# Decoder layer on one core: first output projection, residual, norm and cross-attention queries in one phase that also prepares the key and value weights

## The chip, the cores and the metric

The kernel runs on one core of a Trainium2 chip. The metric is the device time of one execution in microseconds. The core has a matrix engine (TensorE, PE; its weight loads are PEld), a vector engine (VectorE, DVE), a scalar engine (ScalarE, ACT), GpSimd (POOL) and a queue that issues most DMAs (SyncE, SP; SPq in the profile). Line numbers (L356) are those of the kernel before.

## The reference

A decoder layer on 4 sequences of 1024 tokens, width 512, 16 heads, with a context of 2048 tokens:

```python
x = x + attn(layernorm(x), q_heads, k_heads, v_heads, output_proj)      # causal; ends in out @ output_proj.T
x = x + xattn(layernorm(x), ctx, W_q, W_k, W_v, W_o, b_o)               # Q = (..) @ W_q, K = ctx @ W_k, V = ctx @ W_v
x = x + ffn(layernorm(x), gate_W, ..., W1, ..., W2, ...)                # the two best of 4 experts per token
```

## The kernel before

The layer is a row of phases. Each is a block with one instruction stream per engine; all engines meet at its end. The order of the work is written out by hand, and semaphores tie the streams together. The phases: qkv1, self attention, **out1** (`project_out`: attention @ output_proj.T plus residual, stored as x1), **q2** (`project`: x1 is loaded again, normalised, times W_q), **kv2** (`project`: context times W_k and W_v), cross attention, `finish` (last projection, norm, gates), experts.

Tokens go in chunks of 512: eight in out1 and q2, sixteen in kv2. A full-precision product is made of three fast ones: an operand is split into a high part (ACT, a copy to the fast type) and a low part (DVE, the difference), and hi*hi, hi*lo, lo*hi are added up in one PSUM bank. With four slices of the inner width that is 12 matmuls for 128x512 results, here called a tile (of the projection) or a query group.

`load_weights` (L74) loads the weights of a phase, turns them on PE if they are transposed (out1), and splits them in a block of its own; the phase's main block starts when it is over. In `project_out` (L924) a_in, a_hi, a_lo, res and y have two buffers each and the products four PSUM banks. In `project` (L136) DVE makes the statistics of a chunk (L258, L263, L266), POOL the inverse root (L243), DVE the normalised chunk (L273); PE turns it in four pieces (L356, "a turn": four transposes), ACT and DVE split these (L324, L279); PE multiplies (L373; L376 for values), ACT and DVE split the results (L336, L290), SP stores them. The four turns of the next chunk stand between the query groups of this one. x_in has two buffers, and a load goes out when its buffer has been normalised (L153).

`finish` (L1054), which the change leaves alone, has a projection of the same kind (L1463, with two bias matmuls more per tile, L1465 and L1466), with one buffer for a_hi and a_lo (L1285, L1347), two PSUM banks, adds at L1353, statistics from L1326, normalisation on ACT (L1271) and turns at L1479.

## Time and profile before

| | us |
|---|---|
| median of 3 timed runs | 4533.93 (4533.02 to 4535.35) |
| profiled execution | 4499.94 |
| its span | 4498.2 |
| PE, PEld, DVE, ACT, POOL busy | 4079.3, 2522.1, 2722.7, 2096.6, 2476.6 |
| out1, q2, kv2 begin (first DMA issue) | 1084.52, 1198.76, 1347.47 |
| cross attention begins | 1756.16 |

A timeline row has the start, the length, the engine, the line and operation with its output and inputs, how many follow each other, and in brackets the idle time before it with what ended it. In a row of groups the numbers are busy time, mean ns of one, then idle time before and its releasers. In a row of stretches they are the length, the busy time of each engine with its instructions, the granted clock of PE as a share of 2.4 GHz, the share of DMA time, and GB/s. Matmuls overlap, so the distance of starts is the pace, not one matmul's length.

### The profile page before, as it was taken

How to read it: one execution, taken by the hardware profiler on the slowest of the kernel's cores; microseconds unless marked ns; L12 is line 12 of the kernel's file. 1: busy time of each engine (PE TensorE's matmuls, PEld its weight loads, DVE VectorE, ACT ScalarE, POOL GpSimd, SP SyncE). 2: the span in 40 equal slices, each digit the busy share in tenths (PEclk: the TensorE clock that was granted, in tenths of full speed). 3: DMA queues.
4: the chain of work that ended last, by engine and by line, in shares of the span. 5: the costliest groups of instructions: out<-in, count | busy, mean ns of one | idle time of the engine just before them, and what ended most of it. 6: DMA issues, size and time to landing. Idle time of an engine off the chain costs nothing. (4 is left out here: it accounts for less than half of the span.)

```text
span 4498.2 us, 61641 instructions
## 1 busy us (share of the span) xinstructions
PE 4079.3 (91%) x21970; PEld 2522.1 (56%) x21970; DVE 2722.7 (61%) x4947; ACT 2096.6 (47%) x3870; POOL 2476.6 (55%) x931
## 2 busy tenths in 40 slices
PE   6998999997788998999999999999999967549997
PEld 5874555554667886444444444444444346438886
DVE  4436777773453334777777777777777333326765
ACT  2112555554122110566666666666666533226665
POOL 0002334332000001799999999999999915518887
PEclk8996999998899997999999999999999977669998
DMA  4546453522555556022222222222222056134444
GB/s 145 177 155 147 100 109 86 112 47 87 206 189 181 178 171 169 23 57 57 57 58 57 58 58 57 57 58 58 57 57 57 6 189 122 38 99 81 80 83 63
DMA packets 275065, 432.72 MB, mean 96 GB/s; under 512 B 31689, under 2 KB 132041, under 8 KB 268618
## 3 DMA queue, kind: packets, MB, share of 16 engines
q1 hardware_dynamic: 251050, 390.23, 32.6%
q0 software_dynamic: 19776, 36.85, 4.8%
q8 instruction: 161, 2.64, 0.3%
q10 hardware_dynamic: 3968, 2.10, 0.2%
q14 instruction: 110, 0.90, 0.1%
HBM read 258.57 MB, written 170.52 MB: 95 GB/s over the span
## 5 line engine op out<-in xcount | busy, mean ns | idle before, releaser
L881 DVE TENSOR_REDUCE cross_neg_max<-cross_scores 128x1 f32<-128x512 f32 x2048 | 1264.7, 676 | 397.0 <-PE cross_scores L708 396.9
L665 POOL TENSOR_TENSOR cross_partial<-cross_partial,cross_probs 128x2048 f32<-128x2048 f32 x320 | 1465.6, 4580 | 66.7 <-ACT cross_probs L832 29.5
L832 ACT ACTIVATE cross_probs<-cross_shifted 128x512 f32<-128x512 f32 x2048 | 1074.1, 606 | 748.0 <-PE cross_shifted L720 713.8
L708 PE MATMUL cross_scores<-cross_k_stack,cross_q_stack 96*128 96x512 f32 x2048 | 875.6, 437 | 39.5 <-DVE cross_neg_max L881 27.5
L720 PE MATMUL cross_shifted<-cross_q_stack,cross_k_stack 98*128 98x512 f32 x2048 | 850.7, 420 | 15.2 <-DMA cross_q_stack<-cross_neg_dram 6.7
L720 PEld LDWEIGHTS cross_shifted<-cross_q_stack,cross_k_stack 98*128 98x128 f32 x2048 | 387.1, 190 | 388.6 <-issue 239.9
L708 PEld LDWEIGHTS cross_scores<-cross_k_stack,cross_q_stack 96*128 96x128 f32 x2048 | 395.1, 193 | 286.6 <-DVE cross_neg_max L881 224.4
L832 ACT ACTIVATE self_probs<-self_shifted 128x512 f32<-128x512 f32 (+3 forms) x768 | 358.5, 492 | 366.2 <-PE self_shifted L723 285.3
L881 DVE TENSOR_REDUCE self_neg_max<-self_scores 128x1 f32<-128x512 f32 (+3 forms) x768 | 388.2, 547 | 207.1 <-PE self_scores L708 109.5
L736 PE MATMUL cross_out<-cross_probs,cross_v 128*32 128x512 f32 x4096 | 497.2, 603 | 0.0
L708 PE MATMUL self_scores<-self_k_stack,self_q_stack 96*128 96x512 f32 (+3 forms) x768 | 308.6, 423 | 21.7 <-DMA self_k_stack<-k_hi 10.0
L720 PE MATMUL self_shifted<-self_q_stack,self_k_stack 98*128 98x512 f32 (+3 forms) x768 | 298.9, 408 | 11.8 <-issue 11.0
L647 POOL MEMSET cross_neg_max<- 128x128 f32 x1 | 0.2, 210 | 440.9 <-POOLq L1842 440.9
L736 PEld LDWEIGHTS cross_out<-cross_probs,cross_v 128*32 128x32 f32 x4096 | 107.3, 109 | 232.4 <-issue 177.3
L720 PEld LDWEIGHTS self_shifted<-self_q_stack,self_k_stack 98*128 98x128 f32 x768 | 150.9, 198 | 110.8 <-issue 102.6
L663 POOL TENSOR_TENSOR cross_partial<-cross_probs 128x2048 f32<-128x2048 f32 x32 | 146.6, 4580 | 113.6 <-ACT cross_probs L832 113.6
L665 POOL TENSOR_TENSOR self_partial<-self_partial,self_probs 128x2048 f32<-128x2048 f32 (+1 forms) x32 | 128.4, 4014 | 123.1 <-ACT self_probs L832 123.1
L671 POOL TENSOR_TENSOR self_mixed<-self_out_sb,self_inv 128x512 f32<-128x512 f32 x32 | 40.8, 1274 | 281.2 <-issue 281.2
L708 PEld LDWEIGHTS self_scores<-self_k_stack,self_q_stack 96*128 96x128 f32 x768 | 159.6, 208 | 49.3 <-DVE self_neg_max L881 30.0
L1229 POOL DMA_INDIRECT lists<-finish_pairs,finish_place x128 | 134.6, 1051 | 85.2 <-issue 43.4
L901 DVE RECIPROCAL cross_inv<-cross_sum_sb 128x64 f32<-128x64 f32 x256 | 136.7, 539 | 68.4 <-ACT cross_sum_sb L818 68.4
L1724 ACT ACTIVATE experts_t<-experts_t,experts_neg_mean,experts_rstd 128x512 f32<-128x512 f32 x140 | 106.6, 808 | 96.3 <-DVE experts_neg_mean L1801 96.3
(271 smaller groups left out, 6241.5 us busy)
## 6 DMA issues: line engine op xcount, KB each, us to landing
cross_k_stack<-k_hi SPq DMA_DIRECT2D x30, 1024.0 KB, 20.4
kv_x_in<-in_ctx SPq DMA_DIRECT2D x16, 1024.0 KB, 5.5
k_hi<-kv_out_hi SPq DMA_DIRECT2D x64, 256.0 KB, 2.6
k_lo<-kv_out_lo SPq DMA_DIRECT2D x64, 256.0 KB, 3.2
v<-kv_out_n SPq DMA_DIRECT2D x64, 256.0 KB, 2.3
cross_v<-v SPq DMA_DIRECT2D x32, 512.0 KB, 25.1
self_q_stack<-q_hi SPq DMA_DIRECT2D x30, 512.0 KB, 6.9
self_k_stack<-k_hi SPq DMA_DIRECT2D x30, 512.0 KB, 15.6
```

What stands on the lines that cost most here:

```text
L647: pool.memset(neg_max[:, :, :, :], 3.0e38).then_inc(filled.sem, 1)
L663: nc.gpsimd.tensor_tensor(total, probs[:, (e - 1) % PB, :, :], own, ALU.add).then_inc(pool_added.sem, 1)
L665: nc.gpsimd.tensor_tensor(total, total, own, ALU.add).then_inc(pool_added.sem, 1)
L671: nc.gpsimd.tensor_tensor(mixed[:, q % 2], out_sb[:, q % 2], inv[:, :], ALU.mult).then_inc(scaled.sem, 1)
L708: mm = nc.tensor.matmul(scores[at][:, 0:width], q_st[0:96, w, h, q0:q0 + P], k_st[0:96, w, h, half * WIDE:half * WIDE + width], start=True ...
L720: mm = nc.tensor.matmul(shifted[n % SHIFTED][:, f:], k_st[0:98, w, h, kt * P:(kt + 1) * P], q_st[0:98, w, h, qb * QB + f:(qb + 1) * QB], s ...
L736: mm = nc.tensor.matmul(out_ps[32 * h:32 * h + 32, f:], v_sb[:, w, kt, 32 * h:32 * h + 32], probs[:, e % NE % PB, h, f:], start=kt == 0, s ...
L832: nc.scalar.activation(probs[:, e % NE % PB, h, f:], shifted[n % SHIFTED][:, f:], ACT.Exp).then_inc(exped.sem, 1)
L881: nc.vector.tensor_reduce(neg_max[:, q % 2, column(a), half:half + 1], scores[n % (SLOTS * ROUNDS) % AHEAD][:, 0:width], AX.X, ALU.max, ne ...
L901: nc.vector.reciprocal(inv[:, cols], sum_sb[:, cols]).then_inc(inverted.sem, 1)
L1229: pool.indirect_dma_start(lists, bass.IndirectOffsetOnAxis(place[:, t, e:e + 1], 0), pairs[:, t, e, :], None).then_inc(listed, 16)
L1724: nc.scalar.activation(dst[:, t], dst[:, t], ACT.Identity, scale=rstd[:, n, t:t + 1], bias=neg_mean[:, n, t:t + 1]).then_inc(ready, 1)
```

## The change

out1, q2 and the weight part of kv2 become one phase, `bridge`. x1 is stored and stays in SBUF for the norm. a_hi, a_lo, xt_hi, xt_lo have one buffer each, x_in three; the projection has two PSUM banks instead of four. Normalisation moves from DVE to ACT. W_k and W_v are loaded and split in the phase, behind chunks 2 and 4, and `project` takes them ready made; its two first x loads are then the first thing that SP does in kv2. The loops of the two phases become straight code. The helper `after` waits only for values above zero. "Iteration c" is pass c of the loop over the eight chunks; the projections of chunks 0 and 1 stand ahead of it.

```diff
-def project(nc, name, src, chunks, norm, weights, outs, ident, neg_half):
+def project(nc, name, src, chunks, norm, weights, outs, ident, neg_half, split=None):
...
-        load_weights(nc, f"{name}_w", weights, w_hi, w_lo, ident, first_loads)
+        if not split:
+            load_weights(nc, f"{name}_w", weights, w_hi, w_lo, ident, first_loads)
...
+            if split:
+                first_loads(sp)
...
-def project_out(nc, name, attn_t, weight, bias, residual, out, ident):
...
+def bridge(nc, name, attn_t, out_w, residual, x1, q_w, q_out, q_scale, next_w, next_hi, next_lo, ident, neg_half):
...
         a_in = sb("a_in", [P, 2, KT, CH])
+        a_hi = sb("a_hi", [P, KT, CH], F32R)
+        a_lo = sb("a_lo", [P, KT, CH], F32R)
+        x_in = sb("x_in", [P, 3, TPC, D])
+        xt_hi = sb("xt_hi", [P, KT, CH], F32R)
+        xt_lo = sb("xt_lo", [P, KT, CH], F32R)
+        turned = [ctx.enter_context(nc.psum_tensor(f"{name}_turned{n}", [P, KT, P], F32)) for n in range(2)]
+        acc = [ctx.enter_context(nc.psum_tensor(f"{name}_acc{n}", [P, D], F32)) for n in range(2)]
+        q_acc = [ctx.enter_context(nc.psum_tensor(f"{name}_q_acc{n}", [P, CH], F32)) for n in range(HG)]
...
         @block.sync
+            def load_attention(c):
+                after(sp, a_lo_ready, c - 1)
+                sp.dma_start(a_in[:, c % 2], attn_v[c // 2, :, :, c % 2 * CH:(c % 2 + 1) * CH]).then_inc(a_loaded[c % 2], 16)
+            def load(c):
+                if c >= 3:
+                    sp.wait_ge(x_stored[c % 3], 16 * (c // 3))
+                    sp.wait_ge(normed, TPC * (c - 2))
+                sp.dma_start(x_in[:, c % 3], tiles_of(residual)[c]).then_inc(loaded[c % 3], 16)
+            sp.dma_start(raw[:, 0], weight_rows(out_w)).then_inc(raw_loaded[0], 16)
+            load_attention(0)
+            load(0)
+            sp.dma_start(raw[:, 1], weight_rows(q_w)).then_inc(raw_loaded[1], 16)
+            load_attention(1)
+            load(1)
+            load_attention(2)
+            load(2)
+            sp.wait_ge(ow_lo_ready, KT)
+            sp.dma_start(raw[:, 0], weight_rows(next_w[0])).then_inc(raw_loaded[0], 16)
+            sp.wait_ge(qw_lo_ready, 1)
+            sp.dma_start(raw[:, 1], weight_rows(next_w[1])).then_inc(raw_loaded[1], 16)
+            for c in range(CHUNKS):
+                sp.wait_ge(added, TPC * (c + 1))
+                sp.dma_start(tiles_of(x1)[c], x_in[:, c % 3]).then_inc(x_stored[c % 3], 16)
+                if c + 3 < CHUNKS:
+                    load_attention(c + 3)
+                    load(c + 3)
+                for n in range(HG):
+                    sp.wait_ge(out_lo_ready, HG * c + n + 1)
+                    tok = slice(c % 2 * CH, (c % 2 + 1) * CH)
+                    for part, src in ((0, out_hi), (1, out_lo)):
+                        sp.dma_start(q_out[part][c // 2 * HG + n, :, tok], src[:, n].bitcast(F32)).then_inc(q_stored[n], 16)
...
         @block.scalar
+            def attention_high(c):
+                act.wait_ge(a_loaded[c % 2], 16 * (c // 2 + 1))
+                after(act, acc_ready, TPC * c)
+                nc.scalar.activation(a_hi[:, :, :], a_in[:, c % 2], ACT.Copy).then_inc(a_hi_ready, 1)
+            def normalise(c):
+                act.wait_ge(scaled, c + 1)
+                after(act, turned_ready, TPC * (c - 1))
+                for t in range(TPC):
+                    nc.scalar.activation(x_n[:, c % 2, t], x_in[:, c % 3, t], ACT.Identity, scale=rstd[:, t:t + 1],
+                                         bias=shift[:, t:t + 1]).then_inc(normed, 1)
+            def next_high(m):
+                act.wait_ge(raw_loaded[m], 32)
+                nc.scalar.activation(next_hi[:, m], raw[:, m], ACT.Copy).then_inc(next_hi_ready, 1)
...
+            attention_high(0)
+            act.wait_ge(raw_loaded[1], 16)
+            nc.scalar.activation(qw_hi[:, :, :], raw[:, 1], ACT.Copy).then_inc(qw_hi_ready, 1)
+            attention_high(1)
+            normalise(0)
+            attention_high(2)
+            for c in range(CHUNKS):
+                after(act, q_ready, HG * c)
+                for t in range(TPC):
+                    act.wait_ge(turned_ready, TPC * c + t + 1)
+                    nc.scalar.activation(xt_hi[:, :, t * P:(t + 1) * P], turned[t % 2][:, :, :], ACT.Copy).then_inc(hi_ready, 1)
+                if c + 1 < CHUNKS:
+                    normalise(c + 1)
+                if c + 3 < CHUNKS:
+                    attention_high(c + 3)
+                if c in (2, 4):
+                    next_high(c // 2 - 1)
+                for n in range(HG):
+                    act.wait_ge(q_ready, HG * c + n + 1)
+                    after(act, q_stored[n], 32 * c)
+                    nc.scalar.activation(out_hi[:, n], q_acc[n][:, :], ACT.Copy, scale=q_scale).then_inc(out_hi_ready, 1)
         @block.vector
...
+            def attention_low(c):
+                dve.wait_ge(a_hi_ready, c + 1)
+                nc.vector.tensor_tensor(a_lo[:, :, :], a_in[:, c % 2], a_hi[:, :, :].bitcast(F32), ALU.subtract).then_inc(a_lo_ready, 1)
+            def add_projection(c, t):
+                if t == 0:
+                    dve.wait_ge(loaded[c % 3], 16 * (c // 3 + 1))
+                dve.wait_ge(acc_ready, TPC * c + t + 1)
+                nc.vector.tensor_tensor(x_in[:, c % 3, t], acc[t % 2][:, :], x_in[:, c % 3, t], ALU.add).then_inc(added, 1)
+            def variance(c):
+                dve.wait_ge(added, TPC * (c + 1))
...
+            def scales(c):
+                dve.wait_ge(rooted, c + 1)
...
+            def next_low(m):
...
+            attention_low(0)
+            dve.wait_ge(qw_hi_ready, 1)
+            nc.vector.tensor_tensor(qw_lo[:, :, :], raw[:, 1], qw_hi[:, :, :].bitcast(F32), ALU.subtract).then_inc(qw_lo_ready, 1)
+            for t in range(TPC):
+                add_projection(0, t)
+            attention_low(1)
+            variance(0)
+            scales(0)
+            for t in range(TPC):
+                add_projection(1, t)
+            attention_low(2)
+            for c in range(CHUNKS):
+                for t in range(TPC):
+                    dve.wait_ge(hi_ready, TPC * c + t + 1)
+                    nc.vector.tensor_tensor(xt_lo[:, :, t * P:(t + 1) * P], turned[t % 2][:, :, :],
+                                            xt_hi[:, :, t * P:(t + 1) * P].bitcast(F32), ALU.subtract).then_inc(lo_ready, 1)
+                    if t == 0 and c + 1 < CHUNKS:
+                        variance(c + 1)
+                    if t and c + 2 < CHUNKS:
+                        add_projection(c + 2, t - 1)
+                if c + 1 < CHUNKS:
+                    scales(c + 1)
+                if c + 2 < CHUNKS:
+                    add_projection(c + 2, TPC - 1)
+                if c + 3 < CHUNKS:
+                    attention_low(c + 3)
+                if c in (2, 4):
+                    next_low(c // 2 - 1)
+                for n in range(HG):
+                    dve.wait_ge(out_hi_ready, HG * c + n + 1)
+                    after(dve, q_stored[n], 32 * c)
+                    nc.vector.scalar_tensor_tensor(out_lo[:, n], q_acc[n][:, :], q_scale, out_hi[:, n].bitcast(F32),
+                                                   ALU.mult, ALU.subtract).then_inc(out_lo_ready, 1)
         @block.tensor
+            def project_tile(c, t):
+                if t == 0:
+                    pe.wait_ge(a_lo_ready, c + 1)
+                after(pe, added, TPC * c + t - 1)
+                i = 0
+                for part, w in ((a_hi, ow_hi), (a_hi, ow_lo), (a_lo, ow_hi)):
+                    for k in range(KT):
+                        mm = nc.tensor.matmul(acc[t % 2][:, :], part[:, k, t * P:(t + 1) * P], w[:, k, :], start=i == 0, stop=i == 11)
+                        i += 1
+                mm.then_inc(acc_ready, 1)
+            def turn_tile(c, t):
+                pe.wait_ge(normed, TPC * c + t + 1)
+                after(pe, lo_ready, TPC * c + t - 1)
+                for k in range(KT):
+                    mm = nc.tensor.transpose(turned[t % 2][:, k, :], x_n[:, c % 2, t, k * P:(k + 1) * P], ident[:, :])
+                mm.then_inc(turned_ready, 1)
+            def queries(c, n):
+                after(pe, out_lo_ready, HG * (c - 1) + n + 1)
+                i = 0
+                for w, part in ((qw_hi, xt_hi), (qw_hi, xt_lo), (qw_lo, xt_hi)):
+                    for k in range(KT):
+                        mm = nc.tensor.matmul(q_acc[n][:, :], w[:, k, n * P:(n + 1) * P], part[:, k, :], start=i == 0, stop=i == 11)
+                        i += 1
+                mm.then_inc(q_ready, 1)
...
+            for t in range(2 * TPC):
+                project_tile(t // TPC, t % TPC)
+            for c in range(CHUNKS):
+                for t in range(TPC):
+                    turn_tile(c, t)
+                    if t and c + 2 < CHUNKS:
+                        project_tile(c + 2, t - 1)
+                if c + 2 < CHUNKS:
+                    project_tile(c + 2, TPC - 1)
+                pe.wait_ge(lo_ready, TPC * (c + 1))
+                if c == 0:
+                    pe.wait_ge(qw_lo_ready, 1)
+                for n in range(HG):
+                    queries(c, n)
...
-        in_phase(nc, project_out, "out1", attn1, (a["L0_attn_output_proj"], True), None, x, x1, ident)
-        in_phase(nc, project, "q2", x1, 2, True, [(a["L0_xattn_W_q"], False)], [("T", q2[0], q2[1], scale)], ident, neg_half)
-        in_phase(nc, project, "kv2", ctx_in, 4, False, [(a["L0_xattn_W_k"], False), (a["L0_xattn_W_v"], False)],
-                [("T", k2[0], k2[1], 1.0), ("N", v2)], ident, neg_half)
+        with ExitStack() as weights:
+            kv_hi = weights.enter_context(nc.sbuf_tensor("kv2_w_hi", [P, 2, KT, D], F32R))
+            kv_lo = weights.enter_context(nc.sbuf_tensor("kv2_w_lo", [P, 2, KT, D], F32R))
+            kv_w = (a["L0_xattn_W_k"], a["L0_xattn_W_v"])
+            in_phase(nc, bridge, "bridge", attn1, a["L0_attn_output_proj"], x, x1, a["L0_xattn_W_q"], q2, scale, kv_w, kv_hi, kv_lo, ident, neg_half)
+            in_phase(nc, project, "kv2", ctx_in, 4, False, [(w, False) for w in kv_w], [("T", k2[0], k2[1], 1.0), ("N", v2)],
+                     ident, neg_half, (kv_hi, kv_lo))
```

On PE, before, in q2: a turn, a query group, a turn, a query group (out1 was a phase of its own).

```order
L356 MATMUL q_turned<-ident,q_x_n 128x128 x4
L365 REGISTER_ALU
L373 MATMUL q_acc<-q_xt_hi,q_w_hi 128x512 x4
L373 MATMUL q_acc<-q_xt_hi,q_w_lo 128x512 x4
L373 MATMUL q_acc<-q_xt_lo,q_w_hi 128x512 x4
```

On PE now, at the head of iteration 1 of `bridge` (the names of acc are the projection's, of q_acc the queries'; the lines are the new kernel's).

```order
L1180 MATMUL bridge_turned<-ident,bridge_x_n 128x128 x8
L1172 MATMUL bridge_acc<-bridge_ow_hi,bridge_a_hi 128x512 x4
L1172 MATMUL bridge_acc<-bridge_ow_lo,bridge_a_hi 128x512 x4
L1172 MATMUL bridge_acc<-bridge_ow_hi,bridge_a_lo 128x512 x4
L1180 MATMUL bridge_turned<-ident,bridge_x_n 128x128 x4
L1172 MATMUL bridge_acc<-bridge_ow_hi,bridge_a_hi 128x512 x4
```

The turns now stand between tiles of the projection two chunks ahead, and a chunk's query groups follow its own turns. On DVE, before, in q2: statistics of a chunk two ahead between splits.

```order
L290 SCALAR_TENSOR_TENSOR q_out_lo<-q_acc,q_out_hi 128x512
L256 ISA
L258 BN_STATS q_stats<-q_x_in 128x6 x4
L260 ISA
L263 BN_AGGR q_mean_var<-q_stats 128x2 x4
L265 REGISTER_ALU
L266 TENSOR_SCALAR q_var_eps<-q_mean_var 128x4
L278 REGISTER_ALU
L279 TENSOR_TENSOR q_xt_lo<-q_turned,q_xt_hi 128x4x128
```

On DVE now, the head of iteration 0.

```order
L1143 TENSOR_TENSOR bridge_xt_lo<-bridge_turned,bridge_xt_hi 128x4x128
L1108 BN_STATS bridge_stats<-bridge_x_in 128x6 x4
L1112 BN_AGGR bridge_mean_var<-bridge_stats 128x2 x4
L1115 TENSOR_SCALAR bridge_var_eps<-bridge_mean_var 128x4
L1143 TENSOR_TENSOR bridge_xt_lo<-bridge_turned,bridge_xt_hi 128x4x128
L1103 TENSOR_TENSOR bridge_x_in<-bridge_acc,bridge_x_in 128x512
L1143 TENSOR_TENSOR bridge_xt_lo<-bridge_turned,bridge_xt_hi 128x4x128
```

The statistics now stand between the splits of the first and second turned piece, and the projection's adds behind the later ones.

## Rows read from the trace of the kernel before

**Rows 1.** Stretches: length; PE, PEld, DVE, ACT, POOL busy; granted clock, DMA, GB/s.
```profile
1084.52:1198.76 114.24, 93.73 (x400) 77.27 (x400) 41.65 (x41) 17.09 (x9) 0.00 (x0) 0.89 0.66 230
1198.76:1347.47 148.71, 113.58 (x512) 90.54 (x512) 81.75 (x169) 37.90 (x65) 8.07 (x8) 0.87 0.50 177
1347.47:1361.09 13.62, 0.00 (x0) 0.03 (x1) 4.58 (x2) 3.82 (x2) 0.00 (x0) 0.50 0.86 308
```

**Rows 2.** Groups by line, 1084 to 1348: busy, mean ns, idle before, releasers.
```profile
L356 PE MATMUL q_turned<-ident,q_x_n 128*128 128x128 f32 x128 | 22.6, 310 | 36.1 <-DVE q_x_n L273 35.4 <-DVE q_xt_lo L279 0.7
...
L258 DVE BATCH_NORM_STATS2 q_stats<-q_x_in 128x6 f32<-128x512 f32 x32 | 19.7, 679 | 5.9 <-DMA q_x_in<-x 5.3 <-PEq L78 0.6
```

**Rows 3.** Timeline at the edges: start, us, engine, what, idle before, releaser.
```profile
1089.79 3.67 PE L107 MATMUL out_w_turned<-ident,out_w_raw 128*128 128x128 f32 x16 [13.85 <-DMA out_w_raw<-in_L_attn_output_proj]
...
1102.65 2.07 PE L1048 MATMUL out_acc<-out_w_hi,out_a_hi 128*128 128x512 f32 x4 [9.19 <-DVE out_a_lo L1016]
...
1214.02 1.97 PE L356 MATMUL q_turned<-ident,q_x_n 128*128 128x128 f32 x8 [21.31 <-DVE q_x_n L273]
...
1342.42 0.60 ACT L336 ACTIVATE q_out_hi<-q_acc 128x512 fp32r<-128x512 f32 x1 [2.20 <-PE q_acc L373]
...
1347.47 0.40 SPq L92 DMA_DIRECT2D kv_w_raw<-in_L_xattn_W_k  x1
```

**Rows 4.** Landings by source line: L941's load of 1086.05, then L1178's of 3610.90.
```profile
DMA to landing us min/median/max: 11.9/11.9/11.9
...
DMA to landing us min/median/max: 7.7/7.7/7.7
```

**Rows 5.** Groups by line, 1084 to 1348: the attention splits.
```profile
L1016 DVE TENSOR_TENSOR out_a_lo<-out_a_in,out_a_hi 128x2048 fp32r<-128x2048 f32 x8 | 18.2, 2291 | 14.2 <-ACT out_a_hi L1002 14.2
...
L1002 ACT ACTIVATE out_a_hi<-out_a_in 128x2048 fp32r<-128x2048 f32 x8 | 15.2, 1913 | 63.1 <-DMA out_a_in<-attn 45.6 <-PE out_acc L1048 14.6 <-PEq L42 2.9
```

**Rows 6.** Timeline: three query groups leave PE, the first with a turn behind.
```profile
1327.99 0.60 ACT L336 ACTIVATE q_out_hi<-q_acc 128x512 fp32r<-128x512 f32 x1 [2.15 <-PE q_acc L373]
...
1331.22 0.60 ACT L336 ACTIVATE q_out_hi<-q_acc 128x512 fp32r<-128x512 f32 x1 [2.15 <-PE q_acc L373]
...
1334.02 0.60 ACT L336 ACTIVATE q_out_hi<-q_acc 128x512 fp32r<-128x512 f32 x1 [2.20 <-PE q_acc L373]
```

**Rows 7.** Timeline of the last projection's phase, its second chunk.
```profile
3638.55 1.91 ACT L1285 ACTIVATE finish_a_hi<-finish_a_in 128x2048 fp32r<-128x2048 f32 x1 [16.11 <-PE finish_acc L1466]
...
3642.83 2.08 PE L1463 MATMUL finish_acc<-finish_ow_hi,finish_a_hi 128*128 128x512 f32 x4 [4.39 <-DVE finish_a_lo L1347]
...
3647.21 2.93 ACT L1271 ACTIVATE finish_x_n<-finish_x_in,finish_shift,finish_rstd 128x512 f32<-128x512 f32 x4 [6.76 <-DVE finish_rstd_one L1339]
```

**Rows 8.** Stretches there: first tile (14 matmuls) after the wait, and the next.
```profile
3642.83:3648.54 5.71, 5.71 (x14) 4.51 (x15) 3.12 (x11) 1.33 (x2) 1.04 (x1) 0.55 0.61 187
3648.54:3651.72 3.18, 3.18 (x16) 2.63 (x15) 0.69 (x1) 3.15 (x6) 0.00 (x0) 1.00 0.20 77
```

**Rows 9.** Timeline of PE, queries' phase: turns after a long and short wait.
```profile
1255.37 1.11 PE L356 MATMUL q_turned<-ident,q_x_n 128*128 128x128 f32 x4 [2.32 <-DVE q_x_n L273]
...
1260.17 0.60 PE L356 MATMUL q_turned<-ident,q_x_n 128*128 128x128 f32 x4
...
1270.46 0.65 PE L356 MATMUL q_turned<-ident,q_x_n 128*128 128x128 f32 x4 [0.38 <-DVE q_x_n L273]
...
1273.79 0.60 PE L356 MATMUL q_turned<-ident,q_x_n 128*128 128x128 f32 x4
```

**Rows 10.** Timeline of the last projection's phase: statistics, last turn, next matmuls.
```profile
3663.08 2.46 DVE L1326 BATCH_NORM_STATS2 finish_stats<-finish_x_in 128x6 f32<-128x512 f32 x4
...
3666.07 1.28 DVE L1428 TENSOR_TENSOR finish_xt_lo<-finish_turned,finish_xt_hi 128x512 fp32r<-128x512 f32 x2
...
3666.90 1.09 PE L1479 MATMUL finish_turned<-ident,finish_x_n 128*128 128x128 f32 x4 [2.50 <-DVE finish_xt_lo L1428]
...
3669.40 1.87 PE L1488 MATMUL finish_g_ps<-finish_xt_hi,finish_gw_hi 128*4 128x512 f32 x4 [1.41 <-DVE finish_xt_lo L1428]
```

185 lines of the change are left out of this document (88 added, 97 removed).

## The prediction

> **What bounds the kernel now.** I read the table of stretches first, then each engine's waits, then the timeline at the edges of the three phases that the change touches. TensorE (PE) is the busy engine: the first output projection takes 114.24 us with 93.73 busy, the queries' phase 148.71 us with 113.58 busy, and before the first transpose of the keys' and values' phase lie 13.62 us in which PE does nothing [rows 1]. Together that is 276.57 us. The time in which PE idles there has three causes. The starts of the phases: the first projection matmul comes 18.1 us after the phase's first DMA issue, and the queries' first transpose waited 21.3 of the 35.4 us that PE waits for the norm [rows 2, 3]. The norm inside the queries' phase, the other 14 us: three times the statistics waited for x to land, 5.3 us in all [rows 2]. And the weights of keys and values: nothing is multiplied until they are split [rows 1]. VectorE (DVE) is busy 41.65 and 81.75 us in the two phases and bounds neither.
>
> **The change, part by part.** It removes one phase edge, the reload of x1, a weight split ahead of the queries, and the weight split ahead of keys and values. It adds a wait: a_hi and a_lo have one buffer each, so a chunk's split can start only when the projection of the chunk before is done. And it puts the projection's adds, the norm and the queries' splits on one DVE queue. I take it in order of time, from the first DMA issue at 1084.52 [rows 1]. PE is the path unless I say otherwise.
>
> *Start.* Weight landing (5.3 after its issue) and transposes (3.7) are as before, so the transposes are done at 8.9 [rows 1, 3]. The weight's split now goes by quarters; its last copy (0.6) ends at 9.6. The block edge after it is gone, so the first attention split follows on ACT and DVE if its data is there. When that load landed here the trace doesn't say. The same load of the last projection's phase, also second in its queue, landed 7.7 us after its issue, the fourth load of this queue 11.9 [rows 4]. I take 7.7, the same place: 8.1 us from the start, before the copies end. So 9.7 + 1.91 + 2.29 [rows 5] + 0.1 = 14.0 instead of 18.1. The high bound, 11.9, gives 12.3 + 4.3 = 16.6, 2.6 dearer.
>
> *Chunk 0 and chunk 1.* Twelve matmuls are one tile: 14 took 3.18 at the full clock [rows 8], so 2.72 a tile, 10.9 for four. After an idle stretch the first tile runs at the lower level, granted clock 0.55, 1.2 GHz: 5.71 against 3.18, 2.5 more [rows 8]. So 13.4. Then comes the new wait. The last projection's phase has it already: from its a_hi start to the next matmul 4.28 us [rows 7], with 0.25 in front 4.5. Chunk 0 costs 13.4 + 4.5 = 17.9, chunk 1 the same (two turns of 0.44 lie in its 4.5): 35.8.
>
> *Iteration 0.* Four tiles 10.9, four query groups of 2.80 [rows 6] = 11.2, two more turns (3.23 with a turn less 2.80, so 0.43 each) 0.9, and a restart after 3.6 us idle. Rows give 1.6 after 2.3 us [rows 9] and 2.5 after 4.4 [rows 7, 8]; I take 2.0. Sum 25.0.
>
> *Iterations 1 to 5.* Let Q be the end of the previous queries on PE. PE wants turn, turn, tile, turn, tile, turn, tile, tile, queries: 10.9 + 11.2 + 1.8 = 23.8. Does another engine come late? ACT starts 0.25 behind PE and takes 0.6 a piece [rows 6]: the last query group until Q+0.85, the first turned tile until 1.45. DVE takes 0.7 a piece (1.28 for two [rows 10]). It finishes out_lo at 1.6 and xt_lo of tile 0 at 2.3; the third turn comes at 3.6. The statistics with all that follows them (3663.08 to 3666.07, 3.0 [rows 10]) end at 5.3, xt_lo of tile 1 at 6.0; the fourth turn wants it at 6.8. The first add ends at 6.7; the third tile wants its accumulator at 7.2. So PE never waits, with 0.5 to 0.8 to spare. The shift follows at 11.1, the normalisation on ACT (2.93 for four [rows 7]) ends at 14.1, the next a_hi at 16.0, a_lo at 18.3, wanted at 24.7. The split of the next weights (1.9 on ACT, 2.3 on DVE, chunks 2 and 4) fits in there and costs nothing; without that cover it would cost its 4.2. DVE works 14 us of 23.8. SP: storing x1, then waiting for that store to land before the x load, holds the q stores behind it, even at 11.9 [rows 4] no longer than Q+15, and the first is wanted at Q+19. The attention load issued at about Q+2.8 lands at Q+14.7 with 11.9, at 10.5 with 7.7, and its split starts at 14.1; a delay of 6 would still be hidden. Five iterations: 119.2. DMA moves 5 MB (attention, x, x1, twice the queries) in 23.8 us, 210 GB/s, as the projection did with 230 [rows 1].
>
> *Iteration 6* has no tiles between the turns. The fourth turn waits for the statistics: Q+6.0. From there to the queries it took 2.5 in the last phase (turn 3666.90, next matmuls 3669.40) [rows 10]: Q+8.5. With 11.2 and a restart of 2.3: 22.0. *Iteration 7* has no statistics: fourth turn Q+3.0, queries Q+5.3, restart 1.6: 18.1.
>
> *End and keys and values.* From the last matmul to the next phase's first DMA 5.2, as now (1342.42 less 0.25, to 1347.47 [rows 3]). Then PE waits only for its x: a first 1 MB landed 5.3 us after its issue (weight issued 1084.52, transposes 1089.79 [rows 1, 3]); 5.5 instead of 13.62.
>
> Sum: 14.0 + 35.8 + 25.0 + 119.2 + 22.0 + 18.1 + 5.2 + 5.5 = 244.8 against 276.6, a gain of 31.8. Everything behind that is unchanged. The profiled execution took 4499.94 (span 4498.2) and would take 4468.1; the median of the timed runs lies 34.0 above it, and I let that stand: 4533.9 - 31.8 = 4502.1, so 4502. Its own range: the start may cost 2.6 more; the restarts in the iterations (2.0, 2.3, 1.6) may be 1 smaller or 0.5 larger each; the two ends 1 each: 4497 to 4508.
>
> **A rule that speaks against it.** In the last projection's phase, whose tiles go through two accumulators with the same waits, 14 matmuls after the restart ran in 3.18 us at the granted clock 1.00, so at 2.4 GHz [rows 8]; out of the first projection's four accumulators the change makes two. The Trainium skill, page "TensorE: Matmul & The Clock Gate", section "A second HAM failure mode: psum-queue depth-cycling", says that a kernel which cycles accumulator banks can idle briefly between groups so often that the clock swings between its two levels. By that rule the steady tiles would be slow too, the third rival below; the trace so far speaks against it.
>
> **Rivals.**
> 1. *DVE comes late by a little.* The spare time at the fourth turn and third tile is 0.5 to 0.8 us, worked out from durations. If each of six iterations with tiles meets two waits of 1 us, 12 us go: 4514. For: the margins are thin. Against: a wait of 0.37 left the clock up (the next turn came 3.33 later instead of 3.23 [rows 6, 9]), and DVE catches up under the queries.
> 2. *No change.* The same place, but one wait of 2.3 us with its restart of 1.6 [rows 9] in each of six iterations: 23.4, leaving 8.4: 4526. DVE would need 3.1 us more than its rows say.
> 3. *Slower: the clock falls in the tiles.* Each of the 24 tiles inside the loop is entered after a short wait for its accumulator and begins at 1.2 GHz, 2.5 us dearer [rows 8]: 60 more, 28 slower, 4562. It decides the sign from 13 such tiles on. Against it: rows 8, and that in the first two chunks' order an add has a whole tile of the other accumulator, 2.7 us, to be done in.
> 4. *Cheaper restarts.* The three later restarts cost nothing (-5.9): 4496. For: two of those gaps are cut in pieces by turns. Against: a wait of 2.3 already cost 1.6 [rows 9].
>
> That the change does nothing can't be: the 13.62 us of rows 1 lose their cause in any case.
>
> **Chances.** Forecast 0.70, rival 1 0.13, rival 2 0.04, rival 3 0.03, rival 4 0.10. About 0.2% (9 us) is what a measurement of this kernel can tell from no change. Faster by more: 0.70 + 0.13 + 0.10 = 0.93; within: 0.04; slower: 0.03. The range 4491 to 4516 takes in rivals 4 and 1, with a little on either side for what I can't see in the offset of 34.
>
> **What would show it.** Right: the new phase 239 us from its first DMA issue to the next phase's, PE busy 85% or more; two waits of PE for a_lo of 4.3 and about 3.6 us and none for it later; iterations of 23.8; waits for xt_lo only in the last two chunks (about 6 and 3 us); the first transpose of keys and values 5.5 us after its DMA issue. Wrong: PE waits for xt_lo or the adds in iterations 1 to 5 (rivals 1 and 2), a granted clock well below 1 there (rival 3), or ACT waiting for attention beyond Q+20.

## The result, and the profile after

| | us |
|---|---|
| before, median of 4 runs of this comparison | 4533.48 (4530.22 to 4535.35) |
| changed, median of 4 | 4500.01 (4497.48 to 4501.50) |
| ratio | 0.9926, 95% interval 0.9909 to 0.9944 |
| profiled execution of the changed kernel, its span | 4498.85, 4497.1 |

The forecast was 4502.0 with 4491 to 4516 around it. The kernel is faster by 33.5 us where 31.8 were forecast. But the profiled execution is only 1.1 us under the one shown of before, where I had expected 4468.1. Both halves of that need an explanation.

First the bridge, in the profile of the changed kernel. Stretches (length; PE, PEld, DVE, ACT, POOL busy; granted clock, DMA share, GB/s): the whole phase from its first DMA issue to the next phase's, then iterations 1 to 5, iteration 6, and iteration 7 to PE's last matmul.

```profile
1084.27:1323.53 239.26, 207.41 (x912) 167.84 (x912) 114.89 (x191) 82.29 (x111) 8.06 (x8) 0.92 0.54 193
1159.03:1278.80 119.77, 119.77 (x562) 98.22 (x561) 67.56 (x116) 48.08 (x66) 5.03 (x5) 1.00 0.57 202
1278.80:1300.39 21.59, 15.99 (x66) 12.39 (x64) 8.24 (x18) 7.50 (x12) 1.01 (x1) 0.84 0.39 146
1300.39:1318.30 17.91, 15.27 (x65) 11.71 (x63) 5.24 (x8) 4.57 (x8) 0.00 (x0) 0.90 0.47 180
```

The phase takes 239.3 us instead of the 263.0 of its two predecessors [rows 1], PE is busy 87% of it, and in iterations 1 to 5 it is never idle, at the granted clock 1.00 (2.4 GHz).

Next PE's groups of that phase (busy, mean ns, idle before and who ended it). They answer to [rows 2].

```profile
L1172 PE MATMUL bridge_acc<-bridge_ow_hi,bridge_a_hi 128*128 128x512 f32 x128 | 38.8, 427 | 12.8 <-DVE bridge_a_lo L1097 12.8
L1188 PE MATMUL bridge_q_acc<-bridge_xt_hi,bridge_qw_hi 128*128 128x512 f32 x128 | 36.9, 412 | 2.8 <-DVE bridge_xt_lo L1143 2.8
...
L1180 PE MATMUL bridge_turned<-ident,bridge_x_n 128*128 128x128 f32 x128 | 18.2, 275 | 5.4 <-DVE bridge_xt_lo L1143 5.4
```

The 35.4 us that PE waited for the normalised tiles are gone without a rest. In their place stand 12.8 us for a_lo, in three waits, and 8.2 us for xt_lo, all in the last two iterations.

The timeline of PE at the places of [rows 3, 9]: the first matmul of chunk 0, of chunk 1 and of iteration 0's projection, then the two turns that open iteration 1, and the first transposes of keys and values.

```profile
1098.42 2.04 PE L1172 MATMUL bridge_acc<-bridge_ow_hi,bridge_a_hi 128*128 128x512 f32 x4 [4.90 <-DVE bridge_a_lo L1097]
...
1116.55 2.07 PE L1172 MATMUL bridge_acc<-bridge_ow_hi,bridge_a_hi 128*128 128x512 f32 x4 [4.39 <-DVE bridge_a_lo L1097]
...
1134.26 1.70 PE L1172 MATMUL bridge_acc<-bridge_ow_hi,bridge_a_hi 128*128 128x512 f32 x4 [3.52 <-DVE bridge_a_lo L1097]
...
1159.03 1.04 PE L1180 MATMUL bridge_turned<-ident,bridge_x_n 128*128 128x128 f32 x8
...
1329.03 1.97 PE L358 MATMUL kv_turned<-ident,kv_x_in 128*128 128x128 f32 x8 [10.73 <-DMA kv_x_in<-in_ctx]
```

### The profile page after: what moved, and what is told of

It reads as the page before. It is cut to its first block and busy times, and to the rows that moved or that the text cites. A ratio compares the mean times of both kernels' runs of the same rounds, so it can differ in the third digit from the quotient of the medians.

```text
span 4497.1 us, 61153 instructions
## 1 busy us (share of the span) xinstructions
PE 4070.4 (91%) x21970; PEld 2518.9 (56%) x21970; DVE 2708.2 (60%) x4926; ACT 2119.0 (47%) x3905; POOL 2472.1 (55%) x931
## 3 DMA queue, kind: packets, MB, share of 16 engines
q1 hardware_dynamic: 246826, 381.84, 31.8%
## 5 line engine op out<-in xcount | busy, mean ns | idle before, releaser
L722 PE MATMUL self_shifted<-self_q_stack,self_k_stack 98*128 98x512 f32 (+3 forms) x768 | 298.6, 407 | 11.9 <-issue 11.2
```

The costliest lines, as they stand in the source:

```text
L722: mm = nc.tensor.matmul(shifted[n % SHIFTED][:, f:], k_st[0:98, w, h, kt * P:(kt + 1) * P], q_st[0:98, w, h, qb * QB + f:(qb + 1) * QB], s ...
```

## The experiments

Each kernel ran beside the kernel before on the same chip. The medians of the kernel before lie between 4529.85 and 4536.38 from one group of runs to another, and two sets of runs of that same kernel in one group differ by 4.6 us (experiment 1). So a difference of medians under some 5 us is not clear by itself, and such small steps rest on the stretches of the profiles. One group each are before_again, kv_apart, two_planes and stats_2; two_planes_b, late_turns, early_start and stats_4; after_again, listed_4 and listed_wait; and listed_lag_b.

**1. The kernel before once more (before_again).** Nothing is edited.

> The kernel before, unchanged, looked at once more. In the profiled execution shown of it the last-but-one phase (finish) ran 34.5 us a chunk, in the changed kernel's 41 us, and the two profiles are only 1 us apart although the bridge gained 32 us. Theory A: the timed runs of the kernel before (median 4533) have the slower finish too, and the profiled execution (4499.94) was the odd one. Then this profile shows about 4533, sums of TensorE's wait for finish_xt_lo near 89 us and its four finish additions of a chunk not 3.17 us apart. Rival B: the change lengthens the finish phase by moving what stands ahead of it, and the timed 4533 has another source; then this profile shows finish chunks of 34.5 us (a wait sum of 55 us) whatever its time.

Measured: 4531.76 (median of 10), ratio to the other runs of the same kernel 0.9989 (0.9980 to 0.9999), which also tells what a comparison of two equal kernels looks like here. Its profiled execution took 4532.36. Stretches of it: the two replaced phases, keys and values, cross attention, finish.

```profile
1085.30:1346.30 261.00, 204.49 (x912) 165.43 (x912) 123.42 (x210) 55.00 (x74) 8.08 (x8) 0.89 0.58 201
1346.30:1752.80 406.50, 386.18 (x1792) 314.65 (x1792) 134.53 (x194) 77.05 (x130) 0.00 (x0) 0.98 0.55 171
1752.80:3606.30 1853.50, 1787.06 (x9504) 859.86 (x9504) 1385.22 (x2400) 1103.24 (x2112) 1664.72 (x388) 0.98 0.25 56
3606.30:3983.30 377.00, 219.99 (x930) 167.55 (x930) 121.97 (x328) 95.72 (x127) 143.06 (x151) 0.68 0.36 104
```

The last three of these in the changed kernel:

```profile
1323.53:1721.70 398.17, 386.15 (x1792) 314.65 (x1792) 129.83 (x192) 73.19 (x128) 0.09 (x1) 0.99 0.56 169
1721.70:3573.50 1851.80, 1785.99 (x9504) 859.51 (x9504) 1384.20 (x2400) 1102.40 (x2112) 1664.73 (x387) 0.98 0.25 56
3573.50:3949.10 375.60, 218.06 (x930) 167.62 (x930) 121.81 (x328) 95.68 (x127) 142.66 (x151) 0.68 0.37 104
```

And the finish phase in the profile that I forecast from:

```profile
3610.50:3950.40 339.90, 219.70 (x930) 167.55 (x930) 122.03 (x328) 95.69 (x127) 146.86 (x151) 0.70 0.44 115
```

So theory A holds: 377.0 us is the usual length of this phase, 339.9 was the exception; none of its 48 timed runs, here and later (4525.31 to 4540.73), is near the 4499.94 of that execution. PE and DVE are as long busy in one as in the other; what differs is idle time. The 34.0 us that I carried along as an offset are this phase, and not a cost that lies evenly over the program: here it is 37.1 us longer, what stands before it 4.2 shorter, and the two executions differ by 32.4. Against this profile the change reads: 1.0 us before the bridge, 21.7 in it (261.0 to 239.3), 8.3 in keys and values, 1.7 in cross attention, 1.4 in finish, -0.7 in the experts; 33.4 in all, and the two executions differ by 33.5.

Where the idle time sits shows in the four adds of one chunk of finish (L1353 before, L1513 in the changed kernel). Its last two, first in the exceptional profile:

```profile
3753.95 0.69 DVE L1353 TENSOR_TENSOR finish_x_in<-finish_acc,finish_x_in 128x512 f32<-128x512 f32 x1 [2.48 <-PE finish_acc L1466]
3757.12 0.69 DVE L1353 TENSOR_TENSOR finish_x_in<-finish_acc,finish_x_in 128x512 f32<-128x512 f32 x1 [2.48 <-PE finish_acc L1466]
```

Then the last three in the changed kernel's:

```profile
3719.63 0.69 DVE L1513 TENSOR_TENSOR finish_x_in<-finish_acc,finish_x_in 128x512 f32<-128x512 f32 x1 [2.41 <-PE finish_acc L1626]
3725.95 0.69 DVE L1513 TENSOR_TENSOR finish_x_in<-finish_acc,finish_x_in 128x512 f32<-128x512 f32 x1 [5.63 <-PE finish_acc L1626]
3732.32 0.69 DVE L1513 TENSOR_TENSOR finish_x_in<-finish_acc,finish_x_in 128x512 f32<-128x512 f32 x1 [5.68 <-DMA cross_q_stack<-cross_neg_dram]
```

The third and fourth add come 6.3 us after the one before instead of 3.2, for an accumulator that PE, by its own records, had finished:

```profile
3725.55 0.39 PE L1626 MATMUL finish_acc<-finish_bias_lo,finish_first_row 128*128 128x512 f32 x1
3725.87 0.41 PE L1656 MATMUL finish_gt_ps<-ident,finish_g_rows 4*128 4x4 f32 x4
```

The last bias matmul of the fourth tile starts at 3725.55 and PE goes on at once, yet DVE gets the third tile's accumulator at 3725.95 and the fourth's at 3732.32. The releaser named, a DMA of the cross attention, had long been done. The signal is late, or PE's records are early (their ends are modelled); the profile can't tell which. From the fourth chunk on each chunk loses some 6 us in this way, and takes about 41 us instead of 34.5; in five chunks that is most of the 35.7 us by which this phase is longer than in the exceptional profile. Experiments 9 and 10 come back to it.

**2. The weights of keys and values apart (kv_apart).** The second part of the change undone:

```diff
-            sp.dma_start(raw[:, 0], weight_rows(next_w[0])).then_inc(raw_loaded[0], 16)
...
-                if c in (2, 4):
-                    next_high(c // 2 - 1)
...
-                if c in (2, 4):
-                    next_low(c // 2 - 1)
...
-                     ident, neg_half, (kv_hi, kv_lo))
+                     ident, neg_half)
```

> The changed kernel with the weights of keys and values left to their own phase again: the phase of keys and values loads and splits them itself, as before, and the bridge does neither. Theory A, by the terms of my sum: the new phase's first transpose comes 13.6 us after its first DMA issue instead of 5.5, and nothing in the bridge was paid for the preload, so 8.1 us slower than the changed kernel, 4508, and the bridge itself stays at 239. Rival B: the four extra splits (4 x 1.9 on ScalarE, 2 x 2.3 on VectorE) stand on the path in the bridge's third and fifth iteration; then the bridge becomes 2 to 8 us shorter and the loss is 0 to 6 us, 4500 to 4506.

Measured: 4508.97 (4507.86 to 4513.15), 9.0 slower than the changed kernel (ratio to before 0.9944 instead of 0.9926, which would be 8.2). The stretch of keys and values, and PE's first transposes in it:

```profile
1323.47:1731.60 408.13, 387.84 (x1792) 315.97 (x1792) 134.59 (x194) 77.10 (x130) 0.28 (x2) 0.97 0.56 170
```

```profile
1337.01 1.94 PE L358 MATMUL kv_turned<-ident,kv_x_in 128*128 128x128 f32 x8 [18.77 <-DVEq L42]
```

The transposes come 13.54 us after the phase's first issue instead of 5.50: 8.0 of the 8.1 forecast. Iterations 1 to 5 take the same 23.95 us each with and without the splits, so these are hidden. The bridge took 237.2 us; of the 2.0 us by which it is shorter 1.7 lie ahead of iteration 1, where the low clock behind the waits lasted less long. Keys and values pay for it: their stretch is 10.0 us longer, 2 us more than the transposes come late. So this is theory A with about 8 us in the two phases together. So the change's gain divides into 8 to 9 us for the weights and about 25 for the one phase.

**3 and 4. How thin are the margins (stats_2, stats_4)?** Two more statistics instructions (four in stats_4), into a tile that nobody reads:

```diff
+                for t in range(2 if 1 < c < 7 else 0):
+                    nc.vector.bn_stats(more[:, t, :], x_in[:, c % 3, t, :])
                 for t in range(TPC):
                     last = nc.vector.bn_stats(stats[:, t, :], x_in[:, c % 3, t, :])
```

> The changed kernel with the statistics of two tiles taken twice in iterations 1 to 5 of the bridge: 1.2 us more on VectorE just where it is shortest of time. Theory A, by the margins of my forecast (0.5 us ahead of the third tile's accumulator): TensorE now waits some 0.7 us there, the clock stays, 0.7 to 1.2 us an iteration, 3.5 to 6 us in all: 4504 to 4506. Rival B (my third rival): a wait is enough for the clock to fall inside the tiles, 2.5 us and more an iteration on top: 4515 and up. Rival C: the margin is larger than I took it, nothing moves: 4500.

> The changed kernel with four more statistics instructions on VectorE in iterations 1 to 5 (2.5 us instead of the 1.2 us of stats_2). stats_2 cost 0.2 us an iteration, so 1.0 us of its 1.2 us was cover. Theory A: above that cover TensorE pays in full: 1.5 us an iteration, 7.5 us, 4507.5, and the clock stays at full. Rival B (the slower side of my forecast): at waits of this length between tiles the clock falls in each iteration, 2.5 us more each: 4520. Rival C: the wait is taken once and what follows shifts together, as the additions of the next tiles come closer: under 4503.

Measured: 4503.03 and 4507.57. Iterations 1 to 5 in stats_2, then in stats_4, and PE's turns in stats_4:

```profile
1159.44:1280.15 120.71, 120.60 (x561) 97.91 (x560) 72.62 (x126) 48.05 (x66) 5.04 (x5) 1.00 0.56 201
```

```profile
1159.59:1286.25 126.66, 120.60 (x562) 97.90 (x561) 78.51 (x136) 48.04 (x66) 5.05 (x5) 1.00 0.54 191
```

```profile
L1183 PE MATMUL bridge_turned<-ident,bridge_x_n 128*128 128x128 f32 x81 | 11.6, 274 | 6.1 <-DVE bridge_xt_lo L1146 6.1
```

Against 119.77 the iterations cost 0.9 and 6.9 us more. One iteration pays 0.19 for 1.2 us of added work and 1.38 for 2.4: the cover is 1.0 us, where I had worked out 0.8 for the fourth turn. It is the fourth turn that waits first (1.2 us, five times), not the third tile, where stats_2's expectation put it. The granted clock stays 1.00 through all five waits. So stats_4 went by its theory A in the iterations, and stats_2 by its rival C but for a fifth of a microsecond in each. In both profiles the phase of keys and values is longer too, by 2.4 and 2.1 us: its first 22 us ran at a mean granted clock of 0.64 and 0.65, where the changed kernel has 0.79. That stats_4's 4507.57 meets the 4507.5 of its theory so closely is therefore in part chance. The row of stats_2:

```profile
1324.24:1346.24 22.00, 13.92 (x56) 11.20 (x57) 5.44 (x8) 4.67 (x8) 0.00 (x0) 0.64 0.50 168
```

**5 and 6. Two sets of attention planes (two_planes, two_planes_b).** Chunks 1, 3 and 5 are split into the planes of the second weight of keys and values, which are empty until then:

```diff
+        borrowed = lambda c: c in (1, 3, 5)
+        high = lambda c: next_hi[:, 1] if borrowed(c) else a_hi[:, :, :]
+        low = lambda c: next_lo[:, 1] if borrowed(c) else a_lo[:, :, :]
+        reuse = lambda c: c if c == 7 else c - 1
...
-                after(act, acc_ready, TPC * c)
+                after(act, acc_ready, TPC * reuse(c))
```

with a_lo of chunk 1 behind the first add of chunk 0, and of chunk 2 behind the first add of chunk 1.

> The changed kernel with two sets of planes for the split attention in turn (chunks 1, 3 and 5 use the planes of the second weight of keys and values, still empty then), and their splits ordered ahead. Theory A: TensorE's waits for a_lo before chunk 1 (4.4 us) and before the first projection of iteration 0 (3.5 us) go, and with them what the fallen clock costs behind each (1.6 to 2.0 us): 9 to 12 us less, 4488 to 4491. Rival B: VectorE's or ScalarE's next step is late instead (the first normalised tile, the additions), so that half or less is gained: 4494 to 4498.

Measured: 4496.06, 4.0 less than the changed kernel, so rival B; in the profiles the bridge is 6.5 us shorter (232.7). Where chunk 1 ends, the timeline of PE, then of ACT, then of DVE:

```profile
1125.44 2.07 PE L1180 MATMUL bridge_acc<-bridge_ow_hi,kv_w_hi 128*128 128x512 f32 x4 [4.07 <-DVE bridge_x_in L1109]
```

```profile
1117.72 2.93 ACT L1059 ACTIVATE bridge_x_n<-bridge_x_in,bridge_shift,bridge_rstd 128x512 f32<-128x512 f32 x4 [13.44 <-DVE bridge_shift L1126]
1120.56 1.90 ACT L1053 ACTIVATE bridge_a_hi<-bridge_a_in 128x2048 fp32r<-128x2048 f32 x1
```

```profile
1122.49 2.29 DVE L1103 TENSOR_TENSOR bridge_a_lo<-bridge_a_in,bridge_a_hi 128x2048 fp32r<-128x2048 f32 x1 [4.19 <-ACT bridge_a_hi L1053]
1124.70 1.28 DVE L1109 TENSOR_TENSOR bridge_x_in<-bridge_acc,bridge_x_in 128x512 f32<-128x512 f32 x2
```

DVE stood at a_lo for 4.19 us, because on ACT that chunk's high part was queued behind the normalisation; the add behind it was due, and PE waited 4.07 us for it and ran a tile at the lower clock. The wait is that of one queue's order on another's. The mended order:

```diff
-            normalise(0)
             attention_high(2)
+            normalise(0)
...
             add_projection(1, 0)
+            add_projection(1, 1)
             attention_low(2)
-            for t in range(1, TPC):
-                add_projection(1, t)
+            add_projection(1, 2)
+            add_projection(1, 3)
```

> The two sets of planes again, in another order. In the first try two waits went (3.5 of the 4.4 and 3.5 us one by one, and both restarts) and one of 4.1 us came before the last tile of chunk 1: VectorE stood at a_lo of chunk 2 until ScalarE had normalised chunk 0, with the additions behind it. Now ScalarE splits chunk 2 before it normalises chunk 0, and VectorE takes its low part after two additions of chunk 1. Theory A: that wait and the fallen clock behind it (7 us in the records) go and no other comes: phase 227 us instead of 232.7, 4490. Rival B: ScalarE's 1.9 us ahead of the normalisation, or the low part ahead of two additions, make the first turn or the third tile late by as much: 4493 to 4496.

Measured: 4484.78 (4483.54 to 4488.30), 15.2 under the changed kernel, ratio to before 0.9898 (0.9881 to 0.9914). The phase went as theory A says, 226.4 us where 227 were forecast; the median is 5 us under the 4490 of that theory, which the phase doesn't explain. The bridge, its last two iterations, and the first 22 us of keys and values:

```profile
1085.71:1312.06 226.35, 202.34 (x912) 164.44 (x912) 114.45 (x191) 82.41 (x111) 8.06 (x8) 0.94 0.56 205
1267.31:1306.83 39.52, 31.28 (x129) 24.22 (x127) 13.49 (x26) 12.06 (x20) 1.01 (x1) 0.87 0.43 162
1312.06:1334.06 22.00, 14.54 (x67) 11.80 (x68) 6.03 (x9) 5.25 (x9) 0.00 (x0) 0.79 0.58 192
```

Two waits of 7.9 us together and the low clock behind each cost about 12.9 us of the phase.

**7. The last turns between the queries (late_turns).** Chunk 7's tiles are turned between the query groups of chunk 6 and split into a_hi and a_lo, which are free by then:

```diff
                 for n in range(HG):
                     queries(c, n)
+                    if c == LAST - 1:
+                        for t in ((0, 1), (2,), (3,), ())[n]:
+                            turn_tile(LAST, t)
```

with the same interleaving on ACT and DVE.

> On top of the mended two planes: the tiles of the last chunk are turned between the queries of the chunk before it, and split into the planes of the attention, which are free by then. Theory A: the last iteration's waits for xt_lo (1.23 and 1.41 us) and the 3.4 us of fallen clock that followed them go: the last two iterations take 35.5 instead of 39.5 us, 4486. Rival B: the clock falls anyway from the waits of iteration 6 and stays down through the next queries, so only the 2.6 us of waits go: 4487.5 or more. Rival C: ScalarE, now with splits and query evictions in one row, holds the query banks: no gain.

Measured: 4485.63 (4483.96 to 4487.62), no gain. The last two iterations, and the first 22 us of keys and values:

```profile
1269.38:1304.60 35.22, 29.61 (x129) 23.59 (x127) 13.48 (x26) 11.95 (x20) 1.01 (x1) 0.85 0.48 180
1309.83:1331.83 22.00, 14.37 (x58) 11.54 (x59) 5.43 (x8) 4.67 (x8) 0.00 (x0) 0.66 0.51 172
```

The iterations went as theory A says, 35.22 instead of 39.52 us. But the next phase runs its first 22 us at a granted clock of 0.66 instead of 0.79, and took 400.0 instead of 398.0 us; and in this profile the low clock of chunk 0 lasted longer, which cost 1.3 us. So half of the gain in front of the phase edge was given back behind it. That is no chance of one execution: the two profiles of the changed kernel, two_planes and two_planes_b have 0.79 and 398.0 to 398.2 us in that phase, and all five kernels with the late turns have 0.60 to 0.68 and 399.6 to 401.3. stats_2 and stats_4, which have no late turns, are at 0.64 and 0.65 too. Why the clock returns later there is open, and I didn't try what would keep it up. The median meets the 4486 of theory A only because two_planes_b, from which that was counted, came out 5 us lower than forecast.

**8. An early start (early_start).** On top of that, attention chunk 0 is loaded and split ahead of the projection's weight.

```diff
+            load_attention(0)
             sp.dma_start(raw[:, 0], weight_rows(out_w)).then_inc(raw_loaded[0], 16)
-            load_attention(0)
```

> On top of late_turns: the first attention chunk is loaded and split before the weight of the projection, so that its 1.9 and 2.3 us run while the weight lands and is transposed. Theory A: TensorE's 4.9 us wait after the weight's transposes becomes 2.6 and the transposes start 2.5 us later, so the first projection comes 0 to 2 us earlier: within 2 us of late_turns. Rival B: both loads share the queues, the weight lands last and VectorE's four low parts are later than before: 1 to 2 us slower.

Measured: 4482.53 (4480.95 to 4483.89). The timeline of PE, the phase having begun at 1088.80:

```profile
1096.66 3.67 PE L1222 MATMUL bridge_q_acc<-ident,bridge_raw 128*128 128x128 f32 x16 [16.42 <-DMA bridge_raw<-in_L_attn_output_proj]
1101.74 2.07 PE L1198 MATMUL bridge_acc<-bridge_ow_hi,bridge_a_hi 128*128 128x512 f32 x4 [1.41 <-DVE bridge_ow_lo L1147]
```

The transposes start 2.5 us later, the wait behind them shrinks from 4.90 to 1.41, and the first projection comes 12.9 instead of 14.0 us after the first issue. The bridge takes 220.9 us instead of 223.5: 1.0 of the 2.6 lies ahead of the first projection, as theory A allows, 0.8 in chunk 0 and 0.7 from iteration 6's first wait on, in both of which less ran at the low clock. The medians differ by 3.1 and the runs don't overlap, a little beyond theory A; but the two profiled executions took 4483.96 and 4483.89, so more than the one microsecond isn't shown.

**The changed kernel again (after_again).** Nothing is edited.

> The changed kernel, unchanged, once more beside the others of this call. Theory A: the finish phase takes 375 to 377 us as in every profile but the first one of the kernel before (340), the bridge 239, and the time is 4500. Rival B: the quicker finish phase comes now and then by chance, whatever the kernel; then one of the runs could be near 4466.

Measured: 4498.84; in its profile the bridge takes 239.0 and finish 375.3 us. No run of any kernel came near the quicker finish again, so rival B is not excluded, only rare.

**9. What holds back the adds of finish (listed_4, listed_wait)?** In each chunk GpSimd issues 16 small scatters of the token lists, and the late adds come some 14 to 24 us after the first of them. listed_4 gives each expert a semaphore of its own:

```diff
-        listed = sem("listed")
+        listed = [sem(f"listed{e}") for e in range(EXPERTS)]
```

> On top of early_start, in the finish phase: the scatters of the token lists tell of their landing on four semaphores, one for each expert, instead of all on one. In the finish chunks that take 41 us, the last one or two of four additions come up to 7 us late, because TensorE's signal acc_ready comes late, and of the 2048 landing signals of the scatters the trace has 820 to 1025; in the one profile with chunks of 34.5 us it has all 2048. Theory A: the many signals to one semaphore are what holds back TensorE's; spread over four, the chunks come nearer to 34.5 us, 4450 to 4475. Rival B: the stall belongs to the scatters' writes or to all semaphore traffic together, and nothing changes: 4482.

listed_wait lets a tile's four scatters land before the next tile's are issued:

```diff
+                    if t % TPC:
+                        pool.wait_ge(listed, 16 * EXPERTS * t)
```

> On top of early_start, in the finish phase: GpSimd waits, within a chunk, for the four scatters of a tile to have landed before it issues the next tile's. One scatter takes 1.26 us to issue and 5.7 us to land, so this costs GpSimd some 5 us at three places of a chunk, 36 us of scatters instead of 20. Theory A: what holds back TensorE's signal is the pile of scatters not yet landed; with four at most outstanding all four additions of a chunk come 3.17 us apart, and the chunk is bound by GpSimd instead, at 36 + 8 = 44 us, some 20 to 60 us slower. Rival B: the stall is there still (late third or fourth additions) beside GpSimd's longer row: slower by as much or more.

Measured: listed_4 4479.29 (4476.82 to 4484.27), with the adds late as before: rival B. listed_wait 4527.08, one run. GpSimd's waits in one chunk of listed_wait, and DVE's adds over the whole phase:

```profile
3803.24 0.96 POOL L1421 DMA_INDIRECT lists<-finish_pairs,finish_place  x1 [10.98 <-DMA lists<-finish_pairs,finish_place]
...
3811.56 0.96 POOL L1421 DMA_INDIRECT lists<-finish_pairs,finish_place  x1 [3.58 <-DMA lists<-finish_pairs,finish_place]
...
3819.22 0.96 POOL L1421 DMA_INDIRECT lists<-finish_pairs,finish_place  x1 [2.91 <-DMA lists<-finish_pairs,finish_place]
```

```profile
L1545 DVE TENSOR_TENSOR finish_x_in<-finish_acc,finish_x_in 128x512 f32<-128x512 f32 x32 | 21.7, 689 | 80.5 <-PE finish_acc L1658 80.5
```

In early_start the same adds read:

```profile
L1543 DVE TENSOR_TENSOR finish_x_in<-finish_acc,finish_x_in 128x512 f32<-128x512 f32 x32 | 22.1, 691 | 136.5 <-PE finish_acc L1656 89.4 <-DMA cross_q_stack<-cross_neg_dram 31.9 <-issue 15.2
```

The idle time ahead of the adds fell from 136.5 to 80.5 us, and no add was late any more by PE's records, while GpSimd, which waits 17.5 us in this chunk, made the phase 47 us longer. Theory A, though the adds are not 3.17 us apart as it said, since PE itself now starts tiles later.

**10. Eight outstanding at most (listed_lag_b).**

```diff
-        listed = sem("listed")
+        listed = [sem(f"listed{u}") for u in range(2)]
...
+                    if c < 5 and t % TPC >= 2:
+                        pool.wait_ge(listed[t % 2], 16 * EXPERTS * (t // 2))
```

The scatters of even and of odd tiles count on a semaphore each.

> On top of early_start, in the finish phase: GpSimd waits before the third and fourth tile of a chunk for the scatters of the tile before the last to have landed (for the first five chunks alone, whose scatters run beside projections; even and odd tiles have a semaphore each), so that at most eight are outstanding. With four at most (listed_wait) all additions of a chunk came on time again, though GpSimd, waiting 11.0, 3.6 and 2.9 us, had become the bound. Here it waits for the 11 us landing with ten us of issues behind it: 5 to 6 us a chunk, 26 us of scatters and 8 around the root, near 35 us. Theory A: eight outstanding are few enough, the late additions go and a chunk takes 35 to 37 us instead of 40.8: 4450 to 4465. Rival B: the late signals come with eight outstanding too, and the waits are paid on top or hidden: 4480 to 4500.

Measured: 4452.77 (4449.58 to 4456.53), ratio to before 0.9833 (0.9816 to 0.9849): 29.8 under early_start and 47.2 under the changed kernel. The finish phase here (373.4 us in early_start), and its adds:

```profile
3556.80:3903.40 346.60, 218.97 (x930) 167.08 (x930) 122.09 (x328) 95.58 (x127) 147.47 (x151) 0.70 0.40 113
```

```profile
L1546 DVE TENSOR_TENSOR finish_x_in<-finish_acc,finish_x_in 128x512 f32<-128x512 f32 x32 | 22.1, 692 | 113.4 <-PE finish_acc L1659 96.0 <-DMA cross_q_stack<-cross_neg_dram 10.1 <-issue 7.3
```

Theory A again for the time. Of its five throttled chunks GpSimd had to wait in four (once or twice, 2.0 to 11.2 us); in the fifth it never did, and there an add was late again, by 7.6 us:

```profile
3813.06 0.69 DVE L1546 TENSOR_TENSOR finish_x_in<-finish_acc,finish_x_in 128x512 f32<-128x512 f32 x1 [10.12 <-DMA cross_q_stack<-cross_neg_dram]
```

So it is shown that making GpSimd wait takes the late adds away, but not that the number of outstanding scatters is what does it: in the fifth chunk that number was held too. The waits also move the scatters against the adds, and no run tells the two apart.

## Why the forecast was right

| term | forecast | profile |
|---|---|---|
| first issue to first projection | 14.0 | 14.15 |
| chunks 0 and 1, each with its wait | 35.8 | 35.84 |
| iteration 0 | 25.0 | 24.77 |
| iterations 1 to 5 | 119.2 | 119.77 |
| iteration 6 | 22.0 | 21.59 |
| iteration 7 | 18.1 | 17.91 |
| end | 5.2 | 5.23 |
| keys' and values' first transposes | 5.5 | 5.50 |
| sum | 244.8 | 244.76 |

- *Start, chunks 0 and 1.* The load landed 7.8 us after its issue, as the cheap bound had it (7.7). The waits are 4.39 and 3.52 us (4.3 and 3.6 forecast), and experiment 6 shows that they and their low clock are what two buffers would have spared: about 12.9 us, the change's own price for single planes.
- *Iterations 1 to 5.* DVE comes in time at every place. The margin at the fourth turn is 1.0 (experiment 4), not 0.8, and it is the one that breaks first. An iteration takes 23.95, not 23.8, 0.6 us in five.
- *The splits of the next weights* are hidden (experiment 2).
- *Iterations 6 and 7.* 5.60 and 2.64 us of waits for xt_lo; forecast about 6 and 3.
- *End.* The forecast's own terms (1342.42 less 0.25, to 1347.47) give 5.3, not 5.2; a slip of 0.1 that the 5.23 of the profile hides.
- *Rival 1 and 2* needed DVE some 2 to 3 us later than it is: in stats_4, with 2.4 us of added work, a wait of 1.2 us appears in each iteration. *Rival 3*: the steady tiles ran at 1.00, even with a wait of 1.2 us in every iteration. The brief idling between groups, again and again, that the Trainium skill, page "TensorE: Matmul & The Clock Gate", section "A second HAM failure mode: psum-queue depth-cycling", describes for a kernel that cycles through its banks didn't come up here: PE was never idle in iterations 1 to 5 (119.77 us busy of 119.77), two accumulators or not. *Rival 4* (restarts for nothing) is refuted by the same trace: behind the waits of iterations 0, 6 and 7 the low clock cost about 1.6, 2.3 and 1.8 us, against 2.0, 2.3 and 1.6 in the forecast.
- *Failed:* "Everything behind that is unchanged. The profiled execution took 4499.94 (span 4498.2) and would take 4468.1". It took 4498.85. I took the 34.0 us between the profile and the median for an offset that any kernel carries; it was the finish phase of one exceptional execution. Because I worked with a difference and put it on the median, the error fell out of the forecast. The two replaced phases were 2.0 us shorter in the usual profile than in mine, so the gain there was 29.8, and 3.7 us more came from the phases around them. Those 3.7 us are no more than what equal kernels differ by here. That 31.8 met 33.5 so closely is in part chance.

## What to carry to other kernels

Before you forecast from a profile, compare its own time with the timed median; when they differ by more than the runs do, look for the phase in which, since a term read there may belong to that one execution. When two phases become one, add up what each engine's queue owes by each deadline, in order: here that gave every stretch to 0.6 us, and the one order that I did not add up (two_planes) cost a wait of 4 us. A gain just ahead of a phase edge may be given back behind it by the clock (late_turns: 2.0 of 4.3 us).
